# Two states' input products in one GpSimd instruction, pair buffers in place of single ones, in a four-layer fp32 kernel

## The chip, the cores and the metric

The kernel runs on one core of one Trainium2 chip. The metric is the time of one execution on the device in microseconds (us); lower is better. DVE is VectorE, ACT is ScalarE, POOL is GpSimd, PE is TensorE, and SP is SyncE, which here only issues DMAs. Each engine takes its instructions in program order, and engines wait for one another through semaphores.

## The reference

Four layers work on the same 64 x 128 tokens of 192 channels: an embedding with attention, a mixture of experts, a state-space layer run forwards and backwards (`_L1_attn_ref`), and a second mixture of experts. The change touches the state-space layer alone. For each direction it computes, per token t, inner channel d (384 of them) and state n (16):

```python
dt = softplus(dt @ W_dt.T + b_dt); A = -exp(A_log)
dA = exp(dt_t[..., None] * A)                                  # decay
h  = dA * h + (dt_t * x_t)[..., None] * B_t[:, None, :]        # scan over t
y  = einsum('bdn,bn->bd', h, C_t)                              # read with C, sum over n
y_out = 0.5 * (y_fwd + y_bwd) ; out = (y + xc * D) * silu(z) @ W_out.T
```

## The kernel before

`mamba_phase` works through 16 groups of 4 sequences (512 tokens, the free axis of every tile). A group has two halves: d = 0 runs the scan forwards, d = 1 backwards. That makes 32 half-groups, called slots here. A slot has 16 states of 3 channel chunks (DC = 3, 128 partitions each), so 48 units p = 0..47, where n, c = divmod(p, 3).

Each engine has one instruction list, written out unit by unit by `slot` and `program`: at each unit its `main` step, and beside it the steps of the next half's front work (projections, convolution, softplus), placed by the hand-made table `POS`. What a unit costs:

- ACT, `act_decay` (L1644): the decay of one unit, into one of three PSUM banks.
- DVE, `dve_scan` (L1659): the scan of one unit. Its second input is the product u * B in buffer `xh[n % 8]`.
- The product h * C: for 9 of the 16 states by DVE, unit by unit, right behind each scan (`dve_read`, L1668); for the 7 states of `BY_POOL = (0, 3, 4, 7, 10, 12, 15)` by POOL, a whole state in one instruction, in place in `xh` (`pool_read`, L1677).
- PE, `pe_sum` (L1617): adds the products to the output banks, three states behind.
- POOL, `pool_dBx` (L1688): u * B of a whole state (128 x 1536) in one instruction, two states ahead (`AHEAD = 2`).

Every slot's DVE list also holds the three products u of the next slot (`dve_u`, L1564, the last one behind unit 42); POOL's first product of the next slot waits for the last of them. The DVE list of a d = 0 slot holds more: `dve_y` (L1695, units 6, 9, 11), `dve_rows` (L1396, unit 15: it adds the rows of the layer before, in `z`, to `H`, both in SBUF), `dve_out` (L1700, units 19 and 22), and the statistics of the next norm (unit 22), for which POOL waits before `rstd` (L95, unit 23).

B and C come broadcast over the partitions by DMA, two states (QN = 2) in one transfer, into four B buffers and two C buffers (RB = 4, RC = 2). q is the number of a pair of states, 0 to 7. SP issues them in a fixed order: behind the B load of pair q + 2 comes the C load of pair q (`sp_C_in`). The C load of pair q needs the buffer of pair q - 2, and so waits until both states of that pair have been read:

```python
k = (q - RC + 1) * QN
sp.wait_ge(s_prv, s * READS + (reads(k) if k >= 0 else reads(k + NS) - READS))
sp.wait_ge(s_prp, s * POOL_READS + (pool_reads(k) if k >= 0 else pool_reads(k + NS) - POOL_READS))
```

So the C load of pair 1 (states 2 and 3) waits for the read of state 15 of the slot before, and that of pair 3 (states 6 and 7) for POOL's read of state 3.

Of the kernel before, what the change touches and what calls it, by code (L numbers as in the profile page):

```python
# [7 lines left out]
ALU = mybir.AluOpType  # L8
# [7 lines left out]
P = 128  # L16
# [5 lines left out]
TOK = G * P  # L22
# [1236 lines left out]
DC, NS, TAPS, R = 3, 16, 4, 12  # L1259
# [32 lines left out]
def mamba_phase(nc, A, H, bank, K, Y, BCd, W):  # L1292
# [5 lines left out]
    with Phase(nc) as ctx:  # L1298
        sb = lambda n, s, dt=F32: ctx.enter_context(nc.sbuf_tensor(f"m_{n}", s, dt))
        sem = lambda n: ctx.sem(f"m_{n}")  # L1300
        two = range(2)
        NQ, QN = 8, 2
        UNITS = NS * DC
# [10 lines left out]
        BY_POOL = (0, 3, 4, 7, 10, 12, 15)  # L1314
# [19 lines left out]
        u = [sb(f"u{d}", [P, DC, TOK]) for d in two]  # L1334
# [3 lines left out]
        RB, RC = 4, 2  # L1338
        Bb = [sb(f"Bb{b}", [P, QN, TOK]) for b in range(RB)]
        Cb = [sb(f"Cb{b}", [P, QN, TOK]) for b in range(RC)]  # L1340
        NX, AHEAD, LAG = 8, 2, 3
        xh = [sb(f"xh{b}", [P, DC, TOK]) for b in range(NX)]
        ln = LayerNorm(nc, ctx, "m_ln", 1e-5, K)
        s_Ac = sem("A_ready")
        mrs, s_mrs = sb("mrs", [P, G]), sem("mean_rstd")
# [3 lines left out]
        s_BCw, s_B, s_C = sem("BC_written"), [sem(f"B_in{b}") for b in range(RB)], [sem(f"C_in{b}") for b in range(RC)]  # L1349
# [10 lines left out]
        def later(g, d=0):  # L1360
            return not isinstance(g, int) or g > 0 or d > 0
# [20 lines left out]
        def chain(g, d, norm=True, first=False):  # L1382
# [4 lines left out]
            s = g * 2 + d  # L1387
# [147 lines left out]
            def act_w1(act):  # L1535
                act.wait_ge(s_e, s + 1)
                if deep:
                    act.wait_ge(s_dBx, (s - 1) * NS)
                act.activation(w1[d][:, :, :], e[d][:, :, :], ACT.Identity, bias=K.ones[:, 0:1]).then_inc(s_w1, 1)

            def act_ln(act):
# [54 lines left out]
        def at_step(g, d, n):  # L1596

            if n >= NS:
                return (g, 1, n - NS) if d == 0 else (g + 1, 0, n - NS)
            if n < 0:  # L1600
                return (g, 0, n + NS) if d == 1 else (g - 1, 1, n + NS)
            return g, d, n
# [41 lines left out]
            act.activation(o[:, :, lo:hi], seqs(dt[d][:, c, :])[:, :, lo:hi], ACT.Exp, scale=Ac[:, c, n:n + 1]).then_inc(s_dA, 1)  # L1644

        def dve_scan(dve, g, d, p):
            N, U = (g * 2 + d) * NS + p // DC, (g * 2 + d) * UNITS + p
            n, c = divmod(p, DC)
            dve.wait_ge(s_dA, U + 1)
            if c == 0:  # L1650
                dve.wait_ge(s_dBx, N + 1)
            way = slice(None) if d == 0 else slice(None, None, -1)
            if n in BY_POOL:
                o = xh[n % NX][:, c, way]
            else:
                o = bank[:, 6, way]
                if later(g, d) or p > 0:
                    dve.wait_ge(s_prv, (g * 2 + d) * READS + reads(n) + c)
            dve.tensor_tensor_scan(o, bank[:, 3 + p % 3, way], xh[n % NX][:, c, way], 0.0, ALU.mult, ALU.add).then_inc(s_h, 1)  # L1659
# [16 lines left out]
            v = xh[n % NX][:, :, :]  # L1676
            pool.tensor_tensor(v, v, Cb[q % RC][:, n % QN, :].unsqueeze(1).to_broadcast([P, DC, TOK]), ALU.mult).then_inc(s_prp, 1)  # L1677

        def pool_dBx(pool, g, d, n):
            s = g * 2 + d  # L1680
            q = n // QN
            if n == 0:
                pool.wait_ge(s_u, (s + 1) * DC)
            if n % QN == 0:
                pool.wait_ge(s_B[q % RB], (s * (NQ // RB) + q // RB + 1) * 16)
            if later(g, d) or n >= NX:
                pool.wait_ge(s_red, (s * NS + n - NX + 1) * DC)
            pool.tensor_tensor(xh[n % NX][:, :, :], u[d][:, :, :], Bb[q % RB][:, n % QN, :].unsqueeze(1).to_broadcast([P, DC, TOK]),  # L1688
                               ALU.mult).then_inc(s_dBx, 1)

        def dve_y(dve, g, c):
            dve.wait_ge(s_red, (g * 2 * NS + 2 * NS - 1) * DC + c + 1)
# [25 lines left out]
        def sp_B_in(sp, g, d, q):  # L1718
            s = g * 2 + d
            if q == 0:  # L1720
                sp.wait_ge(s_BCw, s * 16 + 16)
            if later(g, d) or q >= RB:
                sp.wait_ge(s_dBx, (s * NQ + q - RB + 1) * QN)
            sp_in(sp, Bb, s_B, 0, d, q)

        def sp_C_in(sp, g, d, q):
# [51 lines left out]
        with nc.Block() as block:  # L1778
            @block.tensor
            def _(pe):  # L1780
                def main(pe, g, d, p, end):
                    carry = d == 0 and later(g)
                    if carry and p in POS["pe_D0"]:
                        pe_D(pe, g, d, POS["pe_D0"].index(p))
                    at_D = POS["pe_D1"] if later(g, d) else (1, 4, 7)
                    if not carry and p in at_D:
                        pe_D(pe, g, d, at_D.index(p))
                    for k in sums_at(carry)[p]:
                        if k >= 0 or later(g, d):
                            pe_sum(pe, *at_step(g, d, k // DC), k % DC)  # L1790
                    if carry and p in POS["pe_out"]:
                        pe_out(pe, g - 1, POS["pe_out"].index(p))

                def after(pe):
                    for n in range(NS - LAG, NS):
                        for c in range(DC):
                            pe_sum(pe, NG - 1, 1, n, c)
                    for i in two:
                        pe_out(pe, NG - 1, i)
                program(pe, "pe", main, lambda pe: None, after)  # L1800

            @block.scalar
            def _(act):
                def main(act, g, d, p, end):
                    act_decay(act, g, d, p)
                program(act, "act", main, lambda act: None, lambda act: None)

            @block.gpsimd
            def _(pool):
                def main(pool, g, d, p, end):  # L1810
                    n, c = divmod(p, DC)
                    if c == 0 and not (end and n >= NS - AHEAD):
                        pool_dBx(pool, *at_step(g, d, n + AHEAD))
                    if c == 1 and (n - 1) % NS in BY_POOL and (n or later(g, d)):
                        pool_read(pool, *at_step(g, d, n - 1))
                def first_dBx(pool):
                    for n in range(AHEAD):
                        pool_dBx(pool, 0, 0, n)
                def last_read(pool):
                    if NS - 1 in BY_POOL:  # L1820
                        pool_read(pool, NG - 1, 1, NS - 1)
                program(pool, "pool", main, first_dBx, last_read)

            @block.vector
            def _(dve):
                def main(dve, g, d, p, end):
                    dve_scan(dve, g, d, p)
                    if p // DC not in BY_POOL:
                        dve_read(dve, g, d, p)
                    if d == 0 and later(g):  # L1830
                        if p in POS["y"]:
                            dve_y(dve, g - 1, POS["y"].index(p))
                        elif p in POS["out"]:
                            dve_out(dve, g - 1, POS["out"].index(p))

                def after(dve):
                    for c in range(DC):
                        dve_y(dve, NG - 1, c)
                    for i in two:
                        dve_out(dve, NG - 1, i)  # L1840
                program(dve, "dve", main, lambda dve: None, after)

            @block.sync
            def _(sp):
                sp_rows(sp, 0)
                sp_BC_out(sp, 0, 0)
                for q in range(RB):
                    sp_B_in(sp, 0, 0, q)
                    if q < RC:
                        sp_C_in(sp, 0, 0, q)  # L1850

                def half(g, d, last):
                    nxt = at_step(g, d, NS)[0:2]
                    end = last and d == 1
                    if d == 0 and not last:
                        sp_rows(sp, g + 1)
                    for q in range(RC, NQ):
                        if q + RB - RC < NQ:
                            sp_B_in(sp, g, d, q + RB - RC)
                        elif not end:  # L1860
                            if q + RB - RC == NQ:
                                sp_BC_out(sp, *nxt)
                            sp_B_in(sp, *nxt, q + RB - RC - NQ)
                        sp_C_in(sp, g, d, q)
                    if not end:
                        for q in range(RC):
                            sp_B_in(sp, *nxt, q + RB - RC)
                            sp_C_in(sp, *nxt, q)

                def group(g, last):  # L1870
                    half(g, 0, last)
                    half(g, 1, last)
                group(0, False)
                with sp.Fori(1, NG - 1) as g:
                    group(g, False)
                group(NG - 1, True)
# [65 lines left out]
```

## Time and profile before

| | before |
|---|---|
| median of 3 runs | 4942.9 us (4937.89 to 4946.77) |
| the profiled execution's own time | 4934.78 us |
| its span, first to last instruction | 4933.0 us |
| busy in the span: PE, DVE, POOL, ACT | 90%, 70%, 65%, 48% |
| the 32 slots of the state-space layer | 1250 to 3984 us of the span |

The span is the time between the first and the last instruction; 1.8 us of the profiled run lie around it. Busy shares are averages over four layers with different limits; in the slots DVE, POOL and PE are all above 90%. The stretches below are taken from the middle of that layer.

### The profile page before, as it was taken

To read this page: it belongs to the slowest core of one execution; us is meant where nothing else is said; L and a number is where in the kernel's file an instruction comes from. 1 tells how busy PE (TensorE), PEld (TensorE's weight loads), DVE (VectorE), ACT (ScalarE), POOL (GpSimd) and SP (SyncE) were. 2 spreads that over 40 slices of the span, in tenths; PEclk is the share of its full clock that TensorE was granted. 3 is DMA by queue.
4 is the path that set the end of the run, shared out by engine and by line. 5 is a ranking of instruction groups with operands and counts; after the bars stand their busy time and mean duration, and the time that the engine had idled before them with its cause. 6 is when DMAs were issued, how large, how long until landed. Compare 5 with 4: busy or idle time off the path is not lost. (4 is left out here: it accounts for less than half of the span.)

```text
span 4933.0 us, 62114 instructions
## 1 busy us (share of the span) xinstructions
PE 4431.2 (90%) x17128; PEld 2288.0 (46%) x17128; DVE 3453.2 (70%) x4958; ACT 2366.7 (48%) x3986; POOL 3229.0 (65%) x1657
## 2 busy tenths in 40 slices
PE   6999987996899999998989899999999877999993
PEld 4666644663334343343333344343434335666662
DVE  4766763111799999999999999999999975111114
ACT  2555542212566666665566566656566534222220
POOL 2222222441899999998989989999999932444441
PEclk9999997997999999999999999999999988999997
DMA  1000012331233233332223232323233211334335
GB/s 30 23 19 19 19 60 63 115 108 51 92 101 109 95 107 106 104 106 97 99 86 107 100 101 98 114 99 103 98 103 104 99 62 56 110 117 117 114 109 186
DMA packets 248101, 444.69 MB, mean 90 GB/s; under 512 B 37292, under 2 KB 162172, under 8 KB 247900
## 3 DMA queue, kind: packets, MB, share of 16 engines
q1 hardware_dynamic: 222556, 390.84, 24.4%
q0 software_dynamic: 25344, 51.94, 3.7%
q14 instruction: 169, 1.38, 0.1%
q8 instruction: 32, 0.52, 0.0%
HBM read 398.90 MB, written 43.78 MB: 90 GB/s over the span
## 5 line engine op out<-in xcount | busy, mean ns | idle before, releaser
L1688 POOL TENSOR_TENSOR m_xh<-m_u,m_Bb 128x1536 f32<-128x1536 f32 x512 | 1761.8, 3471 | 181.1 <-DVE m_u L1564 181.1
L1617 PE MATMUL bank<-m_xh,ident 128*128 128x512 f32 x3072 | 1444.6, 606 | 26.4 <-POOL m_xh L1677 26.4
L1644 ACT ACTIVATE bank<-m_dt,m_Ac 128x508 f32<-128x508 f32 x1536 | 1021.0, 683 | 474.8 <-DVE bank L1659 320.3
L1659 DVE TENSOR_TENSOR_SCAN bank<-bank,m_xh 128x512 f32<-128x512 f32 x864 | 1059.7, 1227 | 34.0 <-ACT bank L1644 7.8
L1617 PEld LDWEIGHTS bank<-m_xh,ident 128*128 128x128 f32 x3072 | 569.1, 192 | 806.3 <-issue 730.9
L1677 POOL TENSOR_TENSOR m_xh<-m_xh,m_Cb 128x1536 f32<-128x1536 f32 x224 | 773.7, 3454 | 8.8 <-DVE m_xh L1659 8.8
L1659 DVE TENSOR_TENSOR_SCAN m_xh<-bank,m_xh 128x512 f32<-128x512 f32 x672 | 771.1, 1201 | 6.6 <-POOL m_xh L1688 3.6
L1668 DVE TENSOR_TENSOR m_xh<-bank,m_Cb 128x512 f32<-128x512 f32 x864 | 597.2, 691 | 68.2 <-DMA m_Cb<-BC_rows 23.0
L1143 ACT ACTIVATE f1t_h<-bank,f1t_b 128x512 f32<-128x512 f32 x234 | 148.2, 684 | 549.6 <-PE bank L1173 549.6
L1075 POOL DMA_INDIRECT rows_y<-f1t_y,f1t_home x156 | 153.7, 985 | 338.5 <-DVE f1t_y L1113 302.9
L1478 PE MATMUL bank<-m_xp,m_dg 128*128 128x512 f32 x768 | 349.6, 597 | 3.3 <-ACT m_xc L1486 2.6
L1182 PE MATMUL bank<-f1t_w,f1t_h 128*128 128x192 f32 x1872 | 314.5, 328 | 16.5 <-ACT f1t_h L1143 16.5
L1182 PEld LDWEIGHTS bank<-f1t_w,f1t_h 128*128 128x128 f32 x1872 | 303.1, 190 | 27.3 <-issue 23.9
L1102 DVE COPY f1t_xTa<-bank 128x512 f32<-128x512 f32 x39 | 27.0, 692 | 361.1 <-PE bank L1154 361.1
L95 POOL TENSOR_SCALAR ln_e_ve<-ln_e_mv 128x4 f32<-128x4 f32 x16 | 3.7, 231 | 362.6 <-DVE ln_e_mv L89 362.6
L1478 PEld LDWEIGHTS bank<-m_xp,m_dg 128*128 128x128 f32 x768 | 144.0, 189 | 195.4 <-issue 167.1
L1170 PE MATMUL bank<-f1t_xTa,f1t_w1a 128*128 128x512 f32 x468 | 229.9, 614 | 1.6 <-DVE f1t_xTb L1105 1.6
L365 DVE TENSOR_REDUCE mx<-bank 128x3 f32<-128x384 f32 x256 | 140.9, 550 | 125.3 <-PE bank L530 124.1
L1113 DVE TENSOR_TENSOR f1t_y<-bank,f1t_b 128x192 f32<-128x192 f32 x156 | 55.8, 357 | 234.8 <-PE bank L1182 234.8
L1062 POOL DMA_INDIRECT f1t_x<-rows_z,f1t_row x156 | 151.0, 968 | 72.7 <-issue 39.1
L1143 ACT ACTIVATE f0t_h<-bank,f0t_b 128x512 f32<-128x512 f32 x114 | 72.2, 684 | 261.4 <-PE bank L1173 261.3
L440 ACT COPY ST<-bank 128x384 f32<-128x384 f32 x256 | 121.1, 473 | 144.2 <-PE bank L540 144.2
(333 smaller groups left out, 6217.2 us busy)
## 6 DMA issues: line engine op xcount, KB each, us to landing
m_Bb<-BC_rows SPq DMA_DIRECT2D x256, 512.0 KB, 4.7
m_Cb<-BC_rows SPq DMA_DIRECT2D x256, 512.0 KB, 3.9
f1t_w<-f_w SPq DMA_DIRECT2D x39, 576.0 KB
f1t_w1a<-f_w SPq DMA_DIRECT2D x39, 384.0 KB
f1c_yg<-rows_y SPq DMA_DIRECT2D x16, 768.0 KB, 8.3
f0t_w<-f_w SPq DMA_DIRECT2D x19, 576.0 KB
f1t_w1b<-f_w SPq DMA_DIRECT2D x78, 96.0 KB
f0t_w1a<-f_w SPq DMA_DIRECT2D x19, 384.0 KB
```

The costliest lines, as they stand in the source:

```text
L1062: pool.indirect_dma_start(x[b][:, j, :], None, Zd, bass.IndirectOffsetOnAxis(row[b][:, j:j + 1].bitcast(U32), 0)).then_inc(s_x[b], 16)
L1075: pool.indirect_dma_start(Y, bass.IndirectOffsetOnAxis(home[b][:, j:j + 1].bitcast(U32), 0), y[b][:, j, :], None).then_inc(s_yout[b], 16)
L1143: act.activation(h[b][:, m, :], bank[:, HB[(s2 + m) % 4], :], ACT.Gelu, bias=b1[b][:, m:m + 1]).then_inc(s_gelu, 1)
L1170: pe.matmul(o[f], w1a[b][:, (m + f) * P:(m + f + 1) * P], xTa[b][:, :], start=True, stop=False)
L1182: mm = pe.matmul(bank[:, YB[j % 2], 0:C], h[b][:, m, j * P:(j + 1) * P], w2[b][:, m, :], start=(m == 0), stop=(m == HK - 1))
L1478: mm = pe.matmul(bank[:, front(c), :], dg[:, c, k, :], xp[:, c, :, o:o + P], start=(k == 0), stop=(k == TAPS - 1))
L1617: mm = pe.matmul(bank[:, c, :], K.ident[:, :], xh[n % NX][:, c, :], start=False, stop=(d == 1 and n == NS - 1))
L1644: act.activation(o[:, :, lo:hi], seqs(dt[d][:, c, :])[:, :, lo:hi], ACT.Exp, scale=Ac[:, c, n:n + 1]).then_inc(s_dA, 1)
L1659: dve.tensor_tensor_scan(o, bank[:, 3 + p % 3, way], xh[n % NX][:, c, way], 0.0, ALU.mult, ALU.add).then_inc(s_h, 1)
L1668: dve.tensor_tensor(xh[n % NX][:, c, :], bank[:, 6, :], Cb[q % RC][:, n % QN, :], ALU.mult).then_inc(s_prv, 1)
L1677: pool.tensor_tensor(v, v, Cb[q % RC][:, n % QN, :].unsqueeze(1).to_broadcast([P, DC, TOK]), ALU.mult).then_inc(s_prp, 1)
L1688: pool.tensor_tensor(xh[n % NX][:, :, :], u[d][:, :, :], Bb[q % RB][:, n % QN, :].unsqueeze(1).to_broadcast([P, DC, TOK]), ALU.mult).then_ ...
```

## The change

The eight `xh` buffers become four pair buffers of two states each; `xh[n]` is now a view of half a pair. `pool_dBx` takes a pair q and forms the products of both its states in one instruction of 128 x 3072, one pair ahead. It is issued at the first unit of each even state (unit 6q issues pair q + 1), in front of the `pool_read` at that state's second unit. Its waits are those of the pair: both buffers must have been summed. `s_dBx` now counts pairs; the waits on it by `act_w1`, `dve_scan` and `sp_B_in` are rewritten for that, and `dve_scan` waits once per pair. The reads, their places, the C loads and all else stay.

```diff
-        xh = [sb(f"xh{b}", [P, DC, TOK]) for b in range(NX)]
+        DBX_AT, READ_AT = 0, 1
+        pairs = [sb(f"xh{b}", [P, QN, DC, TOK]) for b in range(NX // QN)]
+        xh = [pairs[b // QN][:, b % QN, :, :] for b in range(NX)]
@@ act_w1
-                    act.wait_ge(s_dBx, (s - 1) * NS)
+                    act.wait_ge(s_dBx, (s - 1) * NQ)
@@ dve_scan
-            if c == 0:
-                dve.wait_ge(s_dBx, N + 1)
+            if c == 0 and n % QN == 0:
+                dve.wait_ge(s_dBx, s * NQ + n // QN + 1)
@@
-        def pool_dBx(pool, g, d, n):
+        def pool_dBx(pool, g, d, q):
             s = g * 2 + d
-            q = n // QN
-            if n == 0:
+            if q == 0:
                 pool.wait_ge(s_u, (s + 1) * DC)
-            if n % QN == 0:
-                pool.wait_ge(s_B[q % RB], (s * (NQ // RB) + q // RB + 1) * 16)
-            if later(g, d) or n >= NX:
-                pool.wait_ge(s_red, (s * NS + n - NX + 1) * DC)
-            pool.tensor_tensor(xh[n % NX][:, :, :], u[d][:, :, :], Bb[q % RB][:, n % QN, :].unsqueeze(1).to_broadcast([P, DC, TOK]),
-                               ALU.mult).then_inc(s_dBx, 1)
+            pool.wait_ge(s_B[q % RB], (s * (NQ // RB) + q // RB + 1) * 16)
+            if later(g, d) or q >= NX // QN:
+                pool.wait_ge(s_red, (s * NS + (q + 1) * QN - NX) * DC)
+            by_state = u[d][:, :, :].unsqueeze(1).to_broadcast([P, QN, DC, TOK])
+            by_chunk = Bb[q % RB][:, :, :].unsqueeze(2).to_broadcast([P, QN, DC, TOK])
+            pool.tensor_tensor(pairs[q % (NX // QN)][:, :, :, :], by_state, by_chunk, ALU.mult).then_inc(s_dBx, 1)
@@ sp_B_in
-                sp.wait_ge(s_dBx, (s * NQ + q - RB + 1) * QN)
+                sp.wait_ge(s_dBx, s * NQ + q - RB + 1)
@@ gpsimd main
-                    if c == 0 and not (end and n >= NS - AHEAD):
-                        pool_dBx(pool, *at_step(g, d, n + AHEAD))
-                    if c == 1 and (n - 1) % NS in BY_POOL and (n or later(g, d)):
+                    q, i = divmod(p, DC * QN)
+                    if i == DBX_AT and not (end and q == NQ - 1):
+                        pool_dBx(pool, *((g, d, q + 1) if q + 1 < NQ else (*at_step(g, d, NS)[0:2], 0)))
+                    if c == READ_AT and (n - 1) % NS in BY_POOL and (n or later(g, d)):
                         pool_read(pool, *at_step(g, d, n - 1))
                 def first_dBx(pool):
-                    for n in range(AHEAD):
-                        pool_dBx(pool, 0, 0, n)
+                    pool_dBx(pool, 0, 0, 0)
```

## Rows read from the trace of the kernel before

**Rows 1.** Busy time by stretch: a d=1 slot, then two d=0 slots.

```profile
core 0: us, PE busy (x) PEld busy (x) DVE busy (x) ACT busy (x) POOL busy (x), PEclk, DMA share, GB/s
2353.30:2434.40 81.10, 78.07 (x182) 31.51 (x181) 76.80 (x79) 50.96 (x76) 78.30 (x24) 1.00 0.30 101
1919.40:2005.30 85.90, 83.09 (x203) 35.20 (x201) 82.56 (x93) 54.19 (x81) 80.65 (x28) 1.00 0.32 106
2434.40:2534.30 99.90, 84.51 (x202) 36.67 (x201) 96.39 (x93) 54.29 (x81) 79.87 (x27) 0.93 0.27 91
```

**Rows 2.** DVE's waits for C, added up over 1400 to 3900: total, times, longest.

```profile
DVE m_xh L1668 <- DMA m_Cb<-BC_rows: 21.6, 23, 1.5
```

**Rows 3.** Groups by line, engine and shape: count, busy us, mean ns, idle before.

```profile
L1688 POOL TENSOR_TENSOR m_xh<-m_u,m_Bb 128x1536 f32<-128x1536 f32 x512 | 1761.8, 3471 | 181.1 <-DVE m_u L1564 181.1
...
L1677 POOL TENSOR_TENSOR m_xh<-m_xh,m_Cb 128x1536 f32<-128x1536 f32 x224 | 773.7, 3454 | 8.8 <-DVE m_xh L1659 8.8
...
L303 POOL TENSOR_TENSOR xn<-xn,gam 128x768 f32<-128x768 f32 x16 | 29.1, 1816 | 23.2 <-DVE xn L103 23.2
```

**Rows 4.** POOL in order of time, first half of a d=1 slot (from 2353).

```profile
2353.32 10.25 POOL L1688 TENSOR_TENSOR m_xh<-m_u,m_Bb 128x1536 f32<-128x1536 f32 x3 [3.78 <-DVE m_u L1564]
2363.52 3.45 POOL L1677 TENSOR_TENSOR m_xh<-m_xh,m_Cb 128x1536 f32<-128x1536 f32 x1
...
2373.73 10.26 POOL L1688 TENSOR_TENSOR m_xh<-m_u,m_Bb 128x1536 f32<-128x1536 f32 x3
2383.95 3.43 POOL L1677 TENSOR_TENSOR m_xh<-m_xh,m_Cb 128x1536 f32<-128x1536 f32 x1
```

**Rows 5.** SP's issues in the same slot: those of C, out of eight.

```profile
2367.00 0.32 SPq L1716 DMA_DIRECT2D m_Cb<-BC_rows  x1
...
2387.41 0.32 SPq L1716 DMA_DIRECT2D m_Cb<-BC_rows  x1
```

**Rows 6.** DVE in the same slot: scans of states 15, 0, 3, 4, reads of 2, 6.

```profile
2356.80 6.78 DVE L1659 TENSOR_TENSOR_SCAN m_xh<-bank,m_xh 128x512 f32<-128x512 f32 x6
...
2371.49 0.69 DVE L1668 TENSOR_TENSOR m_xh<-bank,m_Cb 128x512 f32<-128x512 f32 x1
...
2376.09 6.78 DVE L1659 TENSOR_TENSOR_SCAN m_xh<-bank,m_xh 128x512 f32<-128x512 f32 x6
...
2391.31 0.69 DVE L1668 TENSOR_TENSOR m_xh<-bank,m_Cb 128x512 f32<-128x512 f32 x1 [1.27 <-DMA m_Cb<-BC_rows]
```

**Rows 7.** DMA issues of the page: KB each, median us to landing.

```profile
m_Cb<-BC_rows SPq DMA_DIRECT2D x256, 512.0 KB, 3.9
```

**Rows 8.** A short d=0 slot (from 1919): POOL, SP and DVE in order of time.

```profile
1919.37 10.23 POOL L1688 TENSOR_TENSOR m_xh<-m_u,m_Bb 128x1536 f32<-128x1536 f32 x3 [2.80 <-DVE m_u L1564]
1929.56 3.45 POOL L1677 TENSOR_TENSOR m_xh<-m_xh,m_Cb 128x1536 f32<-128x1536 f32 x1
...
1949.94 3.44 POOL L1677 TENSOR_TENSOR m_xh<-m_xh,m_Cb 128x1536 f32<-128x1536 f32 x1
1953.34 4.14 POOL L1688 TENSOR_TENSOR m_xh<-m_u,m_Bb 128x1536 f32<-128x1536 f32 x1
...
1933.03 0.32 SPq L1716 DMA_DIRECT2D m_Cb<-BC_rows  x1
...
1937.25 0.69 DVE L1668 TENSOR_TENSOR m_xh<-bank,m_Cb 128x512 f32<-128x512 f32 x1 [0.35 <-DMA m_Cb<-BC_rows]
...
1952.13 2.07 DVE L1396 TENSOR_TENSOR H<-H,m_z 128x768 f32 x1
```

**Rows 9.** A long d=0 slot (from 2434): DVE's row addition, and POOL beside it.

```profile
2467.00 15.75 DVE L1396 TENSOR_TENSOR H<-H,m_z 128x768 f32 x1
...
2475.09 6.84 POOL L1688 TENSOR_TENSOR m_xh<-m_u,m_Bb 128x1536 f32<-128x1536 f32 x2
```

**Rows 10.** The row additions of the loop, all together.

```profile
L1396 DVE TENSOR_TENSOR H<-H,m_z 128x768 f32 x14 | 69.5, 4962 | 0.0
```

**Rows 11.** The layer's start in order of time: DVE's first scans.

```profile
1253.89 3.45 DVE L1659 TENSOR_TENSOR_SCAN m_xh<-bank,m_xh 128x512 f32<-128x512 f32 x3 [3.63 <-POOL m_xh L1688]
```

More of the change, by code:

```diff
@@ L1646, in dve_scan @@
         def dve_scan(dve, g, d, p):
-            N, U = (g * 2 + d) * NS + p // DC, (g * 2 + d) * UNITS + p
+            s, U = g * 2 + d, (g * 2 + d) * UNITS + p
             n, c = divmod(p, DC)
             dve.wait_ge(s_dA, U + 1)
-            if c == 0:
-                dve.wait_ge(s_dBx, N + 1)
+            if c == 0 and n % QN == 0:
+                dve.wait_ge(s_dBx, s * NQ + n // QN + 1)
             way = slice(None) if d == 0 else slice(None, None, -1)
```

## The prediction

> **What bounds the kernel now.** I read the busy shares by stretch first, then the waits, then DVE, POOL and SP in order of time in one slot of each kind. A d=1 slot lasts 81.1 us, of which DVE is busy 76.8, POOL 78.3 and PE 78.1; a d=0 slot lasts 85.9 us when it is short and 99.9 us when it is long [rows 1]. The three engines are so close that only the waits tell who leads. POOL ends each slot idle, waiting for the last u of the next one: 3.78 us ahead of 2353.32 and 2.80 us ahead of 1919.37 [rows 4, 8]. So POOL is not what sets a slot's length; DVE, which makes that u, is. DVE in turn waits in the middle of slots for one thing, a C transfer: 21.6 us in 23 waits over 2500 us [rows 2]. It hardly ever waits for the products themselves: the one such wait that I found is the very first, 3.63 us [rows 11].
>
> Where does C come late from? In the d=1 slot from 2353 POOL's read of state 3 is the row at 2383.95, done at 2387.38. SP issues a C transfer at 2387.41, 0.03 us later, and DVE's read of state 6 starts at 2391.31, 3.90 us after the issue and after 1.27 us of waiting [rows 4, 5, 6]; 3.9 us is also the median landing time [rows 7]. That is the chain read of state 3, C of pair 3, DVE's read of state 6. The chain read of state 15, C of pair 1, DVE's read of state 2 has the same form: POOL's read ends at 2366.97, the issue is at 2367.00, it lands at about 2370.9, and DVE's read starts at 2371.49, so it has 0.6 us to spare there [rows 4 to 6]; in the d=0 slot it has nothing to spare (read ended at 1933.01, issue 1933.03, DVE's read at 1937.25 after 0.35 us of waiting) [rows 8].
>
> The long d=0 slots have another cause. `dve_rows` reads two SBUF tensors. In the short slot it starts at 1952.13 and takes 2.07 us: it ends 0.82 us after POOL's read of state 3 (1949.94 + 3.44), and the POOL instruction begun there shows 4.14 us in place of 3.45 [rows 8]. So it is held while POOL works and goes through at a boundary between two POOL instructions. In the long slot it takes 15.75 us, until 0.82 us after POOL runs out of work (2475.09 + 6.84 = 2481.93) [rows 9]: it missed four boundaries. The 14 additions of the loop sum to 69.5 us [rows 10]; with s of them at 15.7 and the others at about 2.05, s = 3. One miss costs 99.9 - 85.9 = 14.0 us [rows 1].
>
> **The change, part by part.** *The product itself.* A single takes 3.45 us alone and 10.25 us for three, so 3.40 us from start to start [rows 4]. POOL's 128x768 product takes 1.816 us, the 128x1536 one 3.454 us [rows 3]: 2.13 ns for each further column and 0.18 us once. By that a pair takes 3.454 + 1536 x 0.00213 = 6.73 us, and one start in two falls away, less the 0.05 us by which successive ones overlap: I take 0.11 us saved per pair. Bounds: nothing saved (pair = two pitches, 6.80), and 0.17 us saved. The new pattern repeats u over the states and B over the chunks; the rows show no such pattern, and I take it to run as the old one. The Trainium skill (GPSIMD Engine Reference, § Performance versus the Vector engine) measures 4497 ns for 2048 columns, which would make an estimate of 6.75 us for the pair; the sum would not move.
>
> *What 256 x 0.11 = 28 us less POOL work is worth.* Nothing directly: POOL only waits longer for u. It is worth 28 us if POOL is the bound, a rival below.
>
> *The order on POOL.* This is the part that costs. Before, POOL's list from a slot's start is products 0, 1, 2, read 15, product 3, read 0, products 4, 5, 6, read 3, product 7, read 4. After, it is pairs (0,1), (2,3), read 15, read 0, pairs (4,5), (6,7), read 3, read 4. Read 15 now has four products ahead of it where it had three, read 3 eight where it had seven; read 0 and read 4 stand where they stood. So read 15 ends 3.40 - 2 x 0.11 = 3.18 us later and read 3 ends 3.40 - 4 x 0.11 = 2.96 us later, and with each the C transfer behind it on SP, and with that DVE's read. (Read 7 moves likewise, but state 10 is read by POOL, so DVE wants that C only at state 11; read 12 doesn't move.)
>
> *A d=1 slot.* C of pair 1 makes DVE's read of state 2 3.18 - 0.6 = 2.6 us late. C of pair 3 then lands 2.96 us later than now, which is later still than the late DVE; the two don't add, the later one decides: 2.96 us. Nothing behind gives it back, since u, and with it the next slot, follows DVE's order. 16 slots: 47.4 us.
>
> *A short d=0 slot.* DVE's read of state 2 is 3.18 us late (no slack), so `dve_rows` asks at 1952.13 + 3.18 = 1955.3. The first boundary is then the end of read 3, at 1953.38 + 2.96 = 1956.34, and it ends 0.82 us behind that: 1957.16 against 1954.20, 2.96 us later. 11 slots: 32.6 us.
>
> *A long d=0 slot.* There POOL's first 14 pieces set the end of the addition; five pairs among them save 5 x 0.11: 3 slots, -1.7 us.
>
> *The ends.* In slot 0 the first scan waits for a pair where it waited 3.63 us for a single; the read of state 3 is late as elsewhere: 3.0 us. Slot 30, without an addition: 3.2 us.
>
> *Products themselves.* DVE's scans of state 15 and then 0 are one row of six, 6.78 us from 2356.80; those of state 0 begin half of it later, at 2360.2, 6.9 us after POOL's first product; pair (0,1) is ready after 6.73. State 4 begins likewise at 2376.09 + 3.39 = 2379.5, 26.2 us after that product [rows 4, 6]; pair (4,5) is ready after 6 x 3.40 - 0.22 + 6.73 = 26.9, but DVE is 2.6 us late by then. Both are hidden, the first barely: up to 0.2 us per slot, 6 us in all, kept for the range. If C had not made DVE late, (4,5) would cost 0.7 us per d=1 slot. *Buffers:* pair q waits until both states of pair q - 4 are summed; the nearest, (6,7), waits for the sums of state 15, whose read ends 10 us before POOL reaches that pair. *`act_w1`, `sp_B_in`:* same moments in other units; B is loaded four pairs ahead. Nothing for each.
>
> Sum: 47.4 + 32.6 - 1.7 + 3.0 + 3.2 = 84.5 us. Against the profiled execution's own 4934.8 us (span 4933.0 and 1.8 around it) that is 5019.3; its time lies 8.1 us under the median of the runs, so for the median 5027 us.
>
> **What the port can do to this.** Whether `dve_rows` goes through at its boundary is the large unknown. The 11 that went through in the loop all did so, like the one shown, between read 3 and product 7 [rows 8], a boundary that is gone; the new one is between read 3 and read 4. A miss now costs 10.6 us (14.0, less the 2.96 and 0.55 by which hit and miss draw together). All 14 through: 84.5 - 3 x 10.6 = 52.7 us over. All 14 missed: 84.5 + 11 x 10.6 = 201 us over. The Trainium skill (SBUF — State Buffer, § Who interferes with whom) says that a DVE instruction with two SBUF inputs contends with a GpSimd one that reads SBUF, and that the one issued second blocks until the first is done. By that rule every addition gets through at its first boundary, and the time is the 52.7 us case; the trace agrees 11 times in 14 and disagrees three times, where four boundaries passed.
>
> **The rivals.**
> - *Forecast, 58%*: C late by one product, 0 to 6 misses: 4935 + 53 to 4935 + 117, in the median's terms 4995 to 5059.
> - *The new boundary never lets DVE through, 25%*: the same plus up to 11 misses: 4935 + 201 = 5136, 5144 as a median. For it: in the three long slots nine other boundaries all failed, of the kinds product-read, read-product and product-product. Against it: after one miss all later ones may fail by themselves, and first tries succeeded 11 times in 14.
> - *Only part of it arrives, 9%*: PE and ACT, not held by C, catch up and u's waits for them shrink; half of 84.5: about 4985.
> - *The pair costs more than two singles, 3%*: from 0.3 us more each, read 3 is another 1.2 us late: 30 x 1.2 = 36 us more, about 5063.
> - *POOL is the bound after all, 5%; the other side*: then 28 us less of its work come off: 4915. Its mark would be DVE waiting for products or POOL never idle; rows 2 and 4 show the reverse. It decides only if the C transfers are ready before DVE anyway, that is with over 3 us of slack, where the rows show 0.6, 0 and -1.27. The change that saves instruction starts and moves nothing that matters would stand there too.
>
> **How the numbers follow.** What a measurement of this kernel can tell from no change is about 0.2%, 10 us. Faster has the POOL rival, 0.05; same 0.02, of the partly absorbed case; slower the rest, 0.93. Range: below, all additions through, with 0.17 us saved per pair, and some of the partial case: 4985. Above, all missed, with nothing saved per pair (30 x 0.44 = 13 us more): 5155. It is wide because the boundary decides 10.6 us 14 times over; without the case of never, 4985 to 5075.
>
> **What would show it right or wrong.** Right: DVE waits for m_Cb in each slot, some 3 us and more, 90 us and not 22 in sum; POOL's read of state 3 ends 37.3 us after the slot's first product and not 34.1; POOL's wait for u grows to 5 to 6 us per slot; pairs of 6.7 us; d=1 slots of 84.0 us, short d=0 slots of 88.9. Wrong: no waits for C, d=1 slots at 81 us, or scans waiting for m_xh by POOL. How many row additions take over 10 us settles the rest.

## The result, and the profile after

The changed kernel takes 4994.7 us (median of 4 runs, 4990.7 to 5004.0) against 4944.8 us before (4 runs, 4937.9 to 4949.4): a ratio of 1.0105 with a 95% interval of 1.0086 to 1.0124. It is 50 us slower, inside the forecast range of 4985 to 5155, and at its low end: 32 us under the 5027 forecast. The profiled execution took 4994.3 us, 59.5 us more than that of before.

Busy time of the kernel after, in the same columns as [rows 1]: a d=1 slot, a d=0 slot, and one of the shorter d=1 slots.

```profile
core 0: us, PE busy (x) PEld busy (x) DVE busy (x) ACT busy (x) POOL busy (x), PEclk, DMA share, GB/s
1857.90:1943.30 85.40, 80.57 (x182) 32.70 (x181) 76.75 (x79) 51.12 (x76) 77.16 (x16) 0.96 0.31 102
1943.30:2032.00 88.70, 83.75 (x202) 35.12 (x201) 82.28 (x93) 54.13 (x81) 79.51 (x20) 1.00 0.29 97
2380.20:2463.90 83.70, 78.10 (x182) 31.54 (x181) 76.65 (x79) 51.18 (x76) 77.14 (x16) 1.00 0.30 101
```

DVE and POOL are busy for as long as before or less (76.75 and 77.16 us in the d=1 slot against 76.80 and 78.30), in slots that have become longer: what was added for them is waiting. PE is another matter: for the same 182 matmuls it is busy 80.57 us in the first slot and 78.10 in the third, with a granted clock of 0.96 in the one and 1.00 in the other (the section on the prediction comes back to that). The groups and waits of the kernel after name DVE's and POOL's waiting (the group over the whole run, the wait from 1400 to 3960 us); they answer to [rows 2, 3]:

```profile
L1690 POOL TENSOR_TENSOR m_xh<-m_u,m_Bb 128x3072 f32<-128x3072 f32 x256 | 1711.9, 6703 | 256.5 <-DVE m_u L1566 211.1 <-PE bank L1619 44.7 <-DVE bank L1661 0.6
```

```profile
DVE m_xh L1670 <- DMA m_Cb<-BC_rows: 112.2, 43, 3.8
```

DVE waits 112 us for C where it waited 22.5 in the same stretch. POOL did get 50 us of work off (1761.8 to 1711.9 us for the products) and spends it waiting. The kernel after in order of time, in the d=1 slot from 1857.87: POOL, then SP's issues of C, then DVE's two waiting reads; each fence answers to one of [rows 4 to 6].

```profile
1857.87 13.35 POOL L1690 TENSOR_TENSOR m_xh<-m_u,m_Bb 128x3072 f32<-128x3072 f32 x2 [3.89 <-DVE m_u L1566]
1871.18 6.83 POOL L1679 TENSOR_TENSOR m_xh<-m_xh,m_Cb 128x1536 f32<-128x1536 f32 x2
1877.96 13.35 POOL L1690 TENSOR_TENSOR m_xh<-m_u,m_Bb 128x3072 f32<-128x3072 f32 x2
1891.26 6.85 POOL L1679 TENSOR_TENSOR m_xh<-m_xh,m_Cb 128x1536 f32<-128x1536 f32 x2
```

```profile
1874.64 0.32 SPq L1717 DMA_DIRECT2D m_Cb<-BC_rows  x1
...
1894.74 0.32 SPq L1717 DMA_DIRECT2D m_Cb<-BC_rows  x1
```

```profile
1878.69 0.69 DVE L1670 TENSOR_TENSOR m_xh<-bank,m_Cb 128x512 f32<-128x512 f32 x1 [2.83 <-DMA m_Cb<-BC_rows]
...
1898.69 0.69 DVE L1670 TENSOR_TENSOR m_xh<-bank,m_Cb 128x512 f32<-128x512 f32 x1 [1.46 <-DMA m_Cb<-BC_rows]
```

Read 15 is the first of the two at 1871.18; the C issue behind it comes at 1874.64, 16.8 us after the slot's first product, where it came at 13.7. The issue behind read 3 comes at 1894.74, 36.9 us in, where it came at 34.1. Each is followed 4.0 us later by the DVE read that had waited for it.

The row additions, to be set beside [rows 10]:

```profile
L1398 DVE TENSOR_TENSOR H<-H,m_z 128x768 f32 x14 | 23.5, 1682 | 0.0
```

Fourteen of them take 23.5 us in place of 69.5: none was held past its first boundary.

Slot by slot, the lengths between two last u products add the difference up. The 14 d=0 slots from 2 to 28 averaged 89.2 us before, the 11 short ones among them 86.3, and average 88.9 after. The 14 d=1 slots from 3 to 29 went from 81.5 to 85.2 us. So short d=0 slots lost 2.6 us each (11 x 2.6 = 29), the three long ones gained 11 each (-33), and the d=1 slots lost 3.7 each (52). Slots 0, 1, 30 and the tail bring the sum to 59.5. Averages hide that both kinds of slot come in steps; the third part of the section on the prediction takes them apart.

### The profile page after: what moved, and what is told of

Same layout as the page of the kernel before. It is cut to its first block and busy times, and to the rows that moved or that the text cites. A ratio compares the mean times of both kernels' runs of the same rounds, so it can differ in the third digit from the quotient of the medians.

```text
span 4992.6 us, 61370 instructions
## 1 busy us (share of the span) xinstructions
PE 4461.5 (89%) x17128; PEld 2293.7 (46%) x17128; DVE 3404.8 (68%) x4958; ACT 2368.1 (47%) x3986; POOL 3193.3 (64%) x1401
## 5 line engine op out<-in xcount | busy, mean ns | idle before, releaser
L1690 POOL TENSOR_TENSOR m_xh<-m_u,m_Bb 128x3072 f32<-128x3072 f32 x256 | 1711.9, 6703 | 256.5 <-DVE m_u L1566 211.1
L1619 PE MATMUL bank<-m_xh,ident 128*128 128x512 f32 x3072 | 1448.3, 607 | 34.1 <-POOL m_xh L1679 34.1
```

Of the source, the lines that this page charges most:

```text
L1619: mm = pe.matmul(bank[:, c, :], K.ident[:, :], xh[n % NX][:, c, :], start=False, stop=(d == 1 and n == NS - 1))
L1690: pool.tensor_tensor(pairs[q % (NX // QN)][:, :, :, :], by_state, by_chunk, ALU.mult).then_inc(s_dBx, 1)
```

## The experiments

Two theories were set against each other at first (all sums of waits are those from 1400 to 3960 us). *C*: the reads of states 15 and 3 come one product later on POOL, and the C transfers that wait for them make DVE late. *P*: the large instruction itself costs the time, by its wait for two buffers at once (POOL now waits for PE). The kernel before ran again beside every group of experiments, 47 times in all, and each ratio is to its runs in the same group. Those spread widely, from 4889 to 4999 us (median 4942.1); the last two parts of this section are about why.

**Singles in the pairs' order.** The kernel before, with both single products of a pair issued at the even state.

```diff
-                    if c == 0 and not (end and n >= NS - AHEAD):
-                        pool_dBx(pool, *at_step(g, d, n + AHEAD))
+                    if c == 0 and n % QN == 0 and not (end and n >= NS - AHEAD):
+                        for k in range(QN):
+                            pool_dBx(pool, *at_step(g, d, n + AHEAD + k))
```

> The kernel before with its single products, but both of a pair issued at the even state, so POOL's list has the order of the changed kernel and nothing is saved per instruction. Theory C (the reads of states 15 and 3 come one product later, and the C transfers with them): it loses as the changed kernel does and a little more, since each read has 0.2 to 0.4 us less saved ahead of it: 5000 to 5015 us, d=1 slots 85 to 86 us, read of state 3 done 37.4 us after the slot's first product. Theory P (the large instruction itself, its wait for two buffers at once, costs the time): near the kernel before, 4935 to 4950 us.

5061.8 us median (5036 to 5101), ratio 1.0251 (1.0174 to 1.0328). The d=1 slots average 85.5 us, DVE waits 121.0 us for C: the whole loss is there without one large instruction, so P isn't needed for it. The time is above the 5000 to 5015 us that I expected because four row additions in the profiled run missed their boundary (slots of 101.9 us, about 12 us each). That boundary is the one between read 3 and read 4, as in the changed kernel, which missed it in none of its 15.

**Four C buffers under the pairs.** SP's list was rewritten so that a C transfer waits for reads four pairs back; two B buffers were given up for room.

```diff
-        RB, RC = 4, 2
+        RB, RC = 2, 4
...
+                    for j in range(NQ):
+                        b, c = j + RB + 1, j + RC
+                        if b < NQ:
+                            sp_B_in(sp, g, d, b)
+                        elif not end:
+                            sp_B_in(sp, *nxt, b - NQ)
+                        if c < NQ:
+                            sp_C_in(sp, g, d, c)
...
+                            sp_C_in(sp, *nxt, c - NQ)
```

> The changed kernel with four C buffers (and, to pay for them in SBUF, two B buffers in place of four; SP's list is rewritten for that), so that a C transfer waits for reads four pairs back. Theory C: the waits for C vanish, d=0 slots fall from 88.7 to about 85.3, d=1 slots from 85.4 to about 81.5 (the pair of states 4 and 5 is then 0.7 us late): 4890 to 4910 us if the row additions get through. Theory P: 4985 to 5000 us, as the changed kernel, with POOL waiting for PE.

4908.7 us median (4906.2 to 4936.7), ratio 0.9952 (0.9916 to 0.9987); 86 us below the changed kernel. No wait for C is left; busy time of a d=1 and a d=0 slot, columns as above:

```profile
1841.40:1924.10 82.70, 79.77 (x182) 32.10 (x181) 76.91 (x79) 51.06 (x76) 77.17 (x15) 0.98 0.30 103
1924.10:2009.40 85.30, 82.89 (x202) 35.24 (x201) 82.21 (x93) 54.25 (x81) 79.57 (x19) 1.00 0.31 104
```

What is left of the change in a d=1 slot, 82.7 against 81.1, are waits for the products, and a granted clock of 0.98 in place of 1.00. The waits of this kernel:

```profile
DVE bank L1661 <- POOL m_xh L1690: 20.2, 14, 1.5
...
DVE m_xh L1661 <- POOL m_xh L1690: 10.8, 15, 0.7
```

The 0.7 us is the pair (4,5), as worked out in the prediction (0.7 us, if C had not made DVE late). The 1.5 us at the pair (8,9) I had not seen.

**Four C buffers under the singles.** The same edit in the kernel before.

> The kernel before with the same four C and two B buffers. Both theories: only the waits of 1.27 us in each d=1 slot and 0.35 us in each d=0 slot go, some 25 us: 4910 to 4925 us, if again three row additions are held; each one more or less is worth 14 us. If the extra C room is worth as much here as in the changed kernel (over 80 us), C was not what the change lost by.

4941.2 us median (4908.5 to 4990.1), ratio 0.9999 (0.9955 to 1.0042): not the 25 us less that I expected. Its d=1 slots average 81.7 us (81.5 before), though they wait for no C. So the 1.27 us wait for C that I took for the mark of what bounds the slot was covered by something else that is nearly as long. The trace names it: DVE now waits for ACT's decay, 22.1 us in sum where it was 9.0 before; in a d=1 slot that is 0.36 and 0.60 us at two places where the kernel before has no such wait. More room for C is worth 86 us after the change and nothing before it.

**Reads ahead of the pair.** `DBX_AT, READ_AT = 0, 1` becomes `1, 0` in the changed kernel.

> The changed kernel with POOL's read of a state ahead of the pair product at the same place (the read at the first unit of a state, the pair at the second). Theory C: reads of 15 and 3 end 10.4 and 30.6 us after the slot's first product in place of 17 and 37, no waits for C; but the pairs (4,5), (6,7), (8,9) come 3.4 us later and DVE waits for them, about 1.5 us in a d=1 slot: 4900 to 4930 us. Theory P: no gain or worse, 4990 us and up.

4991.6 us median (4990.5 to 4994.9), ratio 1.0085 (1.0042 to 1.0128), against an expected 4900 to 4930. The d=1 slots did what C says: 83.0 us, no wait for C, 0.5 to 0.8 us for each late pair. The d=0 slots got longer, 91.1 us on average. POOL and DVE of this kernel in a d=0 slot:

```profile
1977.13 6.70 POOL L1690 TENSOR_TENSOR m_xh<-m_u,m_Bb 128x3072 f32<-128x3072 f32 x1
1983.76 4.16 POOL L1679 TENSOR_TENSOR m_xh<-m_xh,m_Cb 128x1536 f32<-128x1536 f32 x1
...
1979.44 5.20 DVE L1398 TENSOR_TENSOR H<-H,m_z 128x768 f32 x1
```

DVE asks for its row addition 2.3 us into a pair and has to wait for the end of it: 5.20 us, where it took 1.8 in the changed kernel. That is 3.4 us in each d=0 slot, 48 us in 14, and most of why the gain stayed away. The rest is DVE waiting 51.4 us for pairs, 1.0 us of it in a d=0 slot, and a granted clock that fell in each of these slots (to half for 3.4 or 6.8 us; it did so in 2 of 14 of the changed kernel). So the large instruction does have a price of its own: DVE, if it asks in the middle of a piece, waits for the rest of it, and the piece is twice as long. In the changed kernel DVE asks during a read in all 15 slots, and no such meeting takes place.

**One read moved at a time.** In the changed kernel, only read 15 (then only read 3) goes ahead of the pair at its place (`n == 0` in the first kernel, `n == 4` in the second).

```diff
+                    first = n == 0 and (n or later(g, d))
+                    if c == 0 and first:
+                        pool_read(pool, *at_step(g, d, n - 1))
                     if i == DBX_AT and not (end and q == NQ - 1):
...
-                    if c == READ_AT and (n - 1) % NS in BY_POOL and (n or later(g, d)):
+                    if c == READ_AT and not first and (n - 1) % NS in BY_POOL and (n or later(g, d)):
```

> The changed kernel with one read moved: that of state 15 goes ahead of the pair (2,3), all other places as in the changed kernel. Theory C, by parts: C of pair 1 is early, so d=0 slots (late by that transfer alone) fall from 88.7 to about 86; d=1 slots keep the late C of pair 3 (read of state 3 still done 37 us in) and fall by little, from 85.4 to about 83.5 to 84.5. In all 4925 to 4955 us. If the d=0 slots stay at 88, their cost was not the read of state 15.

4994.9 us median (4992 to 4999): nothing gained, against the 40 to 70 us expected. d=1 slots average 86.1, d=0 slots 88.0. Read 3 ends where it did, 37.2 us after the slot's first product against 36.8: the first C wait is gone and the second has grown to take its place, in the d=1 slot from 1861:

```profile
1894.98 6.84 POOL L1679 TENSOR_TENSOR m_xh<-m_xh,m_Cb 128x1536 f32<-128x1536 f32 x2
...
1902.65 0.69 DVE L1670 TENSOR_TENSOR m_xh<-bank,m_Cb 128x512 f32<-128x512 f32 x1 [3.63 <-DMA m_Cb<-BC_rows]
```

In d=0 slots too DVE, held 1.0 us at state 2 in place of 3.4, runs into a wait of 2.2 to 2.5 us for C at state 6, which I had taken to be on time there. The edit has a price besides: the pairs behind the moved read come late, and DVE waits 30.7 us for them, where no such wait shows in the changed kernel.

> The changed kernel with only the read of state 3 moved ahead of the pair (6,7). C of pair 3 comes 6 us earlier, but C of pair 1 stays late by 3.2 us. d=1 slots: 83.5 to 84.5, late by the 2.6 us of the first transfer. d=0 slots: DVE asks for its row addition 36.2 us in, in the middle of a pair that runs from 30.8 to 37.5, so it ends near 38.3, as in the changed kernel: 88.5 to 89. In all 4965 to 4985 us.

5046.0 us median (5040 to 5056): worse by 51 us, where 10 to 30 us of gain were expected. With C of pair 1 still late, state 3 is scanned late, and POOL now stands in front of its read of state 3 with the pair (6,7) queued behind it:

```profile
1907.19 3.45 POOL L1679 TENSOR_TENSOR m_xh<-m_xh,m_Cb 128x1536 f32<-128x1536 f32 x1 [2.23 <-DVE m_xh L1661]
```

Its d=0 slots (92.7 us) have the row addition at 5.2 us again. Mending either late transfer alone, in this way, gave nothing back; four C buffers mended both and gave 86 us. Since each moved read also makes a pair late, these two runs don't show what one transfer in time would be worth by itself.

**The port taken out.** "Port" stands here, as in the prediction, for what makes DVE's row addition wait for POOL. The row addition is made by POOL at unit 17 of a d=0 slot in place of DVE at unit 15. This is done to the kernel before, to the changed one, and to both with four C buffers.

```diff
-            "rows": 15, "stats": 22, "rstd": 23, "norm": 28, "pe_zT": (44, 47),
+            "rows": 17, "stats": 22, "rstd": 23, "norm": 28, "pe_zT": (44, 47),
...
-                put("dve", at(POS["rows"]), dve_rows)
+                put("pool", at(POS["rows"]), dve_rows)
```

> The kernel before, with the row addition (H += z) made by POOL at unit 17 of a d=0 slot in place of DVE at unit 15. Port theory: that addition being held by POOL is what spreads the kernel before from 4891 to 4987 us; with it off DVE no slot is long, the runs lie within 15 us, and the addition's 2.1 us leave DVE's path too: 4855 to 4880 us. If the long slots have another cause, they stay, and the time stays at 4930 to 4950 us.

> The changed kernel with the row addition made by POOL in the same way. It has no long slots to lose, so only the 1.8 us of the addition leave DVE: about 4970 us (4960 to 4985). Against the run of singles with the addition on POOL it shows what the change costs with the port taken out of both: theory C says 90 to 110 us; if the change cost only what its result shows, 50 us.

> The changed kernel with four C and two B buffers and the row addition on POOL: 4909 us less 14 x 1.8 = 4880 to 4890 us; d=1 slots stay at 82.7, held by pairs that come late. If PE's own work is the floor of a d=0 slot (83 us), not below 84 there.

> Singles with four C and two B buffers and the addition on POOL. In the run of singles with four C buffers the d=1 slots stayed at 81 to 82 us though their 1.27 us waits for C were gone, so C was hidden there: I expect the same time as the singles with the addition on POOL and two C buffers, within 5 us. If it is 20 us lower, C did cost something in the kernel before.

| row addition on POOL | two C buffers | four C buffers |
|---|---|---|
| singles | 4883.7 (4881.5 to 4884.4) | 4883.4 (4881.0 to 4885.3) |
| pairs | 4970.4 (4962.9 to 4982.0) | 4900.7 (4897.9 to 4913.0) |

The ratios to the kernel before are 0.9874 (0.9812 to 0.9935), 0.9873 (0.9811 to 0.9934), 1.0056 (1.0021 to 1.0091) and 0.9933 (0.9897 to 0.9970), in the order singles two, singles four, pairs two, pairs four. One execution of pairs with two C buffers took 18197 us and is left out of its range; without it the median would be 4970.0.

Three things follow. With the port out of the way the kernel before runs within 3 us, not within 110, and is 58 us faster (4942.1, the median of its 47 runs, less 4883.7): the held additions were its spread. The change costs 4970.4 - 4883.7 = 86.7 us. And 69.6 of these go with two more C buffers, which do nothing for the singles (0.3 us). I read the other 17 as pairs that are formed late: DVE waits 31 us for them with pairs and four C buffers, and 0.5 us with singles. No run was made for that, and part of it comes from the clock, which fell for 3.4 us in all 14 of these d=1 slots with pairs and in 1 of 14 with singles.

Two of the four times came out as expected: pairs with two C buffers (4970 us), and singles with four C buffers as with two. The others did not: the singles took 4883.7 against 4855 to 4880, the cost of the change was 86.7 against 90 to 110, and pairs with four C buffers took 4900.7 against 4880 to 4890: DVE gave up 1.8 us in each d=0 slot there and got a new wait of 1.2 us for PE in front of `dve_out`. The singles with the addition on POOL are the fastest version found, 1.3% under the kernel before.

**Why pairs miss no boundary.** Two kernels ask whether it matters what stands ahead of the boundary or behind it. In each one pair of the changed kernel is made as two singles: (6,7) in the first (`q == 3`), (8,9) in the second (`q == 4`).

```diff
+            if q == 3:
+                for i in range(QN):
+                    op = pool.tensor_tensor(pairs[q % (NX // QN)][:, i, :, :], u[d][:, :, :],
+                                            Bb[q % RB][:, i, :].unsqueeze(1).to_broadcast([P, DC, TOK]), ALU.mult)
+                op.then_inc(s_dBx, 1)
+                return
```

> The changed kernel with the pair (6,7), the last product ahead of the boundary at which DVE's row addition gets through, made as two single products. So far kernels of pairs missed that boundary 0 times in 45 profiled tries, kernels of singles 9 times in 45. If a pair in front of it is what helps, misses of some 10 us each come back: 1 to 5 in 14, 5000 to 5050 us and a spread of tens of us. If not, 4990 to 5000 us.

> The changed kernel with the pair (8,9), the first product behind that boundary and the read of state 4, made as two singles. If what lies behind the boundary (how much POOL has lined up) decides, misses come back here and not in the run with (6,7) split: 5000 to 5050 us with a spread of tens of us. If not, 4990 to 5000 us.

5008.1 us median (4997 to 5039) with (6,7) split, one miss in 15 additions; 5004.9 (5002 to 5012) with (8,9) split, none. That is too little to tell the two apart. But the ten profiles in which DVE makes the addition can be laid together by another measure, the time from DVE's start of the addition to POOL's next boundary:

| start to next boundary, us | additions | held past it |
|---|---|---|
| 0.28 to 0.86 | 44 | 0 |
| 0.86 to 1.05 | 29 | 1 |
| 1.05 to 1.48 | 36 | 9 |
| 1.48 to 5.0 | 41 | 0 |

Nine of the ten misses fall in one stretch: 3 of 11 additions there in the kernel before, 3 of 9 in the singles in the pairs' order, 2 of 13 in the singles with four C buffers, 1 of 2 with (6,7) split, 0 of 1 with (8,9) split. The tenth, at 0.865 us, is in the singles in the pairs' order. The stretch isn't enough by itself: 27 of its 36 additions got through, in the kernel before one of them at 1.336 us, between misses at 1.316, 1.337 and 1.338. The kernel before starts its additions 0.77 to 1.46 us ahead of the boundary, the changed one 0.61 to 1.00 (but for the first of all, at 2.65 and 2.26). So what the change did to the additions goes with where it put DVE's start: out of the stretch in which boundaries are missed. That is a correlation, and I drew the stretches after seeing the numbers. The kernels differ in more than this start, and kernels of pairs had only three additions in that stretch, so that nothing here shows whether pairs help by themselves. Why a boundary is missed stays open.

## Why the prediction was right, and where its size was off

**The mechanism held.** The order on POOL was named as the part that costs, with the two chains from reads 15 and 3 through C to DVE's reads of states 2 and 6. Moving the products of the kernel before into that order, with nothing else changed, gives the loss; taking the wait for C away takes most of it back, 69.6 of 86.7 us. The marks came out so: C waits of 112 us (forecast 90), read 3 done 36.8 us after the slot's first product (37.3), pairs of 6.70 us (6.73), short d=0 slots of 88.7 (88.9). Two marks came out otherwise: d=1 slots mostly of 85.4 us (84.0), and POOL's wait for u at 4.7 us per slot in the mean (5 to 6).

**The sum, with the port out, was some 10% too high.** The 84.5 us forecast count three long slots that gain 0.6 us each. With the addition on POOL there are none; with 2.96 us for each of the 14 the same terms give 47.4 + 41.4 + 3.0 + 3.2 = 95.0 us, and 86.7 were measured. That 84.5 lies so close to 86.7 is luck.

**d=1 slots: 2.96 us forecast, 3.7 measured, and the missing term is PE's clock.** "The two don't add, the later one decides" was right for DVE's own waits: DVE's read of state 2 starts 20.82 us after the slot's first product (18.17 before), its read of state 6 40.82 us after it (37.99 before), so 2.65 and then 2.83 us late. Up to 61 us into the slot the d=1 slots of the changed kernel run alike. Then PE stands idle for some 3.3 us, waiting for ACT's `m_u`, and in 13 of 14 slots the granted clock falls to half (1.2 GHz in place of 2.4) in that idle time or, once, 0.2 us behind it. PE's sums for the next slot's `m_dt` behind it take longer, and what waits for them is late. Busy time of the same 6.8 us in the slot from 1857 and in the shorter one from 2380:

```profile
1918.80:1925.60 6.80, 5.84 (x8) 2.51 (x8) 6.63 (x7) 4.14 (x6) 6.13 (x2) 0.52 0.78 224
2441.10:2447.90 6.80, 5.83 (x14) 2.72 (x15) 6.63 (x7) 5.08 (x8) 6.27 (x3) 1.00 0.61 224
```

In the same busy time PE makes 8 matmuls in place of 14. The first slot from there to its end:

```profile
1927.99 6.70 POOL L1690 TENSOR_TENSOR m_xh<-m_u,m_Bb 128x3072 f32<-128x3072 f32 x1 [2.52 <-PE bank L1619]
...
1934.57 0.69 DVE L1566 TENSOR_TENSOR m_u<-bank,m_xc 128x512 f32<-128x512 f32 x1 [0.83 <-ACT m_dt L1562]
...
1942.30 0.69 DVE L1566 TENSOR_TENSOR m_u<-bank,m_xc 128x512 f32<-128x512 f32 x1 [1.12 <-ACT m_dt L1562]
```

The slot from 2380 has neither the 2.52 nor the 0.83, and 0.34 in place of the 1.12. The slot lengths go by how long the clock was at half (each row a kind of slot and its kernel, the 14 d=1 slots from 3 to 29 or the short ones of the d=0 slots from 2 to 28):

| granted clock at half for | 0 us | 3.4 us | 6.8 us |
|---|---|---|---|
| d=1, before | 9 slots of 81.1 us | 5 of 82.2 | none |
| d=1, after | 1 of 83.7 | 2 of 84.3 | 11 of 85.5 |
| d=0 (short), before | 8 of 85.9 | 3 of 87.4 | none |
| d=0, after | 12 of 88.7 | 2 of 90.2 | none |
| d=1, pairs, addition on POOL | 5 of 83.7 | 7 of 84.3 | 2 of 85.7 |

So at full clock a d=1 slot lost 2.6 us, somewhat less than the 2.96 forecast, and the rest of the 3.7 is the clock. The forecast had no term for it: its step "nothing behind gives it back" was right, but something behind took more. PE's idle time at that place was 2.7 us before, and the clock fell behind it in 5 of 14 slots; after, it was 3.2 to 3.5 us. Why the clock falls in one slot and not in the next, with the same idle time, the runs don't show.

**d=0 slots: 2.96 forecast, 2.6 measured.** The chain was right, DVE's read of state 2 waits 3.43 us and the addition ends at the first boundary. At full clock the loss is 2.8 us (85.9 to 88.7); the average is smaller because the clock fell in 3 of 11 short slots before and in 2 of 14 after. The saving per pair was 0.15 us and not 0.11: two pairs take 13.35 us, so 6.65 from start to start against 2 x 3.40, and four pairs ahead of read 3 make that 0.16 us.

**What bounds the kernel: half right.** DVE's wait for C in [rows 6] was read as what held the d=1 slot. The run of singles with four C buffers shows that it held nothing: the slot is as long without it, with waits for ACT's decay in its place. It was still the right place to look, since it was the wait with no room left. The sizes came out all the same because C's lateness is measured from DVE's need and not from a bound. (That DVE, POOL and PE are all above 90% busy in the slots holds for the short ones; in the long slot of [rows 1] POOL and PE are at 80 and 85%.)

**The port: the term that decided the number.** The forecast kept about three misses in 14 after as before, and put the case of none at 52.7 us over. It was none: 59.5 us over between the two profiled runs, 50 in the medians. So this term, three misses at 10.6 us, takes 32 us off the 84.5 and makes the range's low end the right place. The clock puts about 14 us on, and the slots that lost a little less at full clock than forecast take 7 off (14 x 0.36 + 11 x 0.16): about 60 us, where 59.5 were measured. That the medians lie 32 us under the forecast, by just the size of the one term, is in part two errors that cancel, and in part how many additions the other runs of the kernel before missed, which no profile shows. The rival that the new boundary never lets DVE through (25%) was wrong: it did so 15 times in 15. The Trainium skill's rule (SBUF — State Buffer, § Who interferes with whom), that the one issued second blocks until the first is done, fitted the changed kernel throughout, 15 additions of 15; the kernel before breaks it, where DVE was passed over at four boundaries in a row. Nor is the new boundary safe by itself: the singles in the pairs' order have the same one and missed it 4 times in 15.

**POOL as the bound: refuted.** Its products cost 50 us less and its wait for u grew by 30 (181.1 us in [rows 3], 211.1 in the row of it above). Nothing came of it.

## What to carry to other kernels

A larger instruction on an in-order engine is also a reordering: everything behind it moves by a whole piece, so list for each of those what frees a buffer and which transfer waits for it, even where the merged instruction itself is cheaper. Of two transfers late by the same cause the later one decides; mending the first alone gained nothing here. When a slot is longer than its waits explain, look at PE's granted clock in it before looking for another wait: two slots of the same kernel differed by 1.7 us for that alone. And before judging a change of 1%, look whether its own runs differ by more than that: here an addition of 2 us on DVE, held by GpSimd in some slots of some runs, spread the time before over 110 us, and moving it to GpSimd was worth 58 us.

## What the runs showed of the hardware that I had not expected

- A DVE addition with both inputs in SBUF, held by GpSimd, goes through at the first boundary between two GpSimd instructions or at none: in the ten profiles 10 of 150 additions missed their first boundary, and every one of them then missed all others too (1 to 3 more) and ended only when GpSimd had run out of work, in the shown slot 0.82 us after it [rows 9]. Nine of the ten started 1.05 to 1.48 us ahead of the boundary, and so did 27 that got through; why that should matter the runs don't show.
- GpSimd pays 0.7 us where DVE gets in: the piece begun at that boundary shows 4.15 us in place of 3.45. DVE's addition ends 0.81 to 0.82 us behind the last piece that held it, in all 150.
- On GpSimd the pattern with two repeats (u over the states, B over the chunks) runs as fast as the one with a single repeat: 6.70 us for 3072 columns against 3.45 for 1536. Merging two instructions saves 0.15 us.
- PE's granted clock, at full before, fell to half for 3.4 or 6.8 us at one idle gap of an otherwise busy slot (PE busy 78 of 81 us): in 5 of 14 d=1 slots before, 0.4 to 1.5 us behind a gap of 2.7 us, and in 13 of 14 after, mostly within a gap of 3.2 to 3.5 us. A d=1 slot got 1.1 us longer by it before and up to 1.8 us after.
